# Staged rows laid out by channel group, small pieces of the experts' loads, and work moved between engines at the seams of a three-stage kernel

## The reference

```
h = concat(patches @ W + b, table[x_txt])
h = h + causal_attention(layernorm(h))
h = h + ternary_ffn(layernorm(h))                  # gelu, width 1024
x = layernorm(h); xi, z = split(x @ Win.T)         # 512 channels each
lam = exp(-8 softplus(omega) sigmoid(xi @ Wl.T + bl));  v = xi @ Wv.T + bv
h_t = lam_t (h_{t-1} - 2 v_t (v_t . h_{t-1}) / |v_t|^2) + (1 - lam_t) xi_t    # 192 steps
h = h + (silu(z) * h_t) @ Wout.T
h = h + moe(layernorm(h))     # 8 experts, 2 per token
```

## Time and profile before

| | us |
|---|---|
| median of 3 runs | 997.94 (995.04 to 998.17) |
| the profiled execution | 999.17 |
| its span, first to last instruction | 997.4 |
| TensorE busy | 942.3 (94%) |
| VectorE busy | 785.9 (79%) |
| ScalarE busy | 594.5 (60%) |
| GpSimd busy | 542.2 (54%) |
| transfers | 96.34 MB in 135878 packets, 130166 of them under 2 KB |

### The profile page before, as it was taken

How to read it: one execution, slowest core, us unless ns; L and a number is a source line. 1 busy time by engine, 2 the same in 40 slices (tenths; PEclk the granted TensorE clock), 3 DMA queues, 4 the chain that set the end, 5 groups by cost and what they waited for, 6 DMA issues and landing times. The chain is left out here.

```text
span 997.4 us, 19802 instructions
## 1 busy us (share of the span) xinstructions
PE 942.3 (94%) x6006; PEld 844.9 (85%) x6006; DVE 785.9 (79%) x2396; ACT 594.5 (60%) x1181; POOL 542.2 (54%) x662
## 2 busy tenths in 40 slices
PE   6889999999999999988799999999998999997998
PEld 6789999999999999875588888888887888876887
DVE  4877777777777777664499999999997889995776
ACT  1366666666666666563567676777664666752541
POOL 4256666666666666344355455555543446542663
PEclk9999999999999999899899999999999899999999
DMA  6001111111111141003799999999999999993210
GB/s 221 17 27 43 44 43 43 42 42 42 42 42 42 42 149 32 17 17 111 89 149 156 156 156 154 156 154 155 155 154 173 145 153 145 150 143 76 98 64 22
DMA packets 135878, 96.34 MB, mean 97 GB/s; under 512 B 12270, under 2 KB 130166, under 8 KB 135158
## 3 DMA queue, kind: packets, MB, share of 16 engines
q1 hardware_dynamic: 134262, 91.20, 53.4%
q0 software_dynamic: 1536, 4.20, 1.4%
HBM read 31.91 MB, written 13.11 MB: 45 GB/s over the span
## 5 line engine op out<-in xcount | busy, mean ns | idle before, releaser
L334 POOL TENSOR_TENSOR gelu_lo<-gelu_out,gelu_hi 128x384 fp32r<-128x384 f32 x124 | 145.6, 1200 | 34.0 <-DVE gelu_hi L549 32.1
L1036 POOL TENSOR_TENSOR B_y<-B_scan_in,B_states 128x512 f32<-128x512 f32 x48 | 61.8, 1288 | 97.8 <-ACT B_states L1110 97.8
L752 PE MATMUL psAB<-ternary_down,gelu_hi 128*128 128x256 f32 x384 | 96.7, 290 | 4.9 <-POOL gelu_lo L334 4.0
L688 PE MATMUL psAB<-x2T_hi,ternary_up 128*128 128x384 f32 x256 | 94.9, 371 | 2.5 <-DVE residual L678 2.3
L752 PE MATMUL psAB<-ternary_down,gelu_lo 128*128 128x256 f32 x384 | 93.3, 282 | 0.0
L688 PE MATMUL psAB<-x2T_lo,ternary_up 128*128 128x384 f32 x256 | 87.9, 343 | 0.0
L1284 PE MATMUL psAB<-Win_hi,B_x_hi 128*128 128x512 f32 x192 | 83.5, 435 | 0.0
L1296 PEld LDWEIGHTS psAB<-B_partial_dots,B_minus_same_batch 128*128 128x128 f32 x384 | 65.3, 191 | 18.2 <-DVE B_partial_dots L1187 9.2
L752 PEld LDWEIGHTS psAB<-ternary_down,gelu_hi 128*128 128x128 f32 x384 | 72.2, 188 | 8.9 <-POOL gelu_lo L334 7.5
L1203 DVE SCALAR_TENSOR_TENSOR psAB<-B_decayed_u,psAB 128x128 f32<-128x128 f32 x192 | 68.0, 354 | 12.7 <-PE psAB L1296 11.5
L1284 PE MATMUL psAB<-Win_hi,B_x_lo 128*128 128x512 f32 x192 | 75.7, 394 | 0.0
(11 more groups left out here) (267 smaller groups left out, 3330.4 us busy)
## 6 DMA issues: line engine op xcount, KB each, us to landing
B_scan_in<-B_stage SPq DMA_DIRECT2D x192, 256.0 KB, 6.6
patches<-in_patches SPq DMA_DIRECT2D x16, 384.0 KB, 3.1
B_residual<-layer_out SPq DMA_DIRECT2D x48, 128.0 KB, 3.5
out_dram<-B_residual SPq DMA_DIRECT2D x48, 128.0 KB, 2.8
layer_out<-residual SPq DMA_DIRECT2D x32, 128.0 KB, 1.8
raw_Win<-in_experts SPq DMA_DIRECT2D x4, 768.0 KB, 4.4
raw_Wl<-in_experts SPq DMA_DIRECT2D x4, 768.0 KB, 4.1
layer_out<-residual SPq DMA_DIRECT2D x32, 64.0 KB, 2.0
```

The source lines that it names most:

```text
L334: nc.gpsimd.tensor_tensor(act_l[:, k, :], act[:, k % DEEP, :], act_h[:, k, :].bitcast(F32), ALU.subtract).then_inc(s["ffn_lo"], 1)
L688: last = nc.tensor.matmul(out, a, b, start=(n == 0), stop=(n == len(terms) - 1))
L752: last = nc.tensor.matmul(ps[:, 6 + k // 2, (k % 2) * D:(k % 2 + 1) * D], x[:, c, k * P:(k + 1) * P], dn_w[:, c, :], start=(c == 0 and x i ...
L1036: nc.gpsimd.tensor_tensor(y[:, j % 2], ring[:, j % R_RING, :, GATE, :], hs[:, j % 2], ALU.mult).then_inc(s["y"], 1)
```

## The change

It writes `stage` as slot, channel group, quantity, channel, so that each copy into the ring reads one run of 2 KB per partition; spreads the loads for stage C over iterations 22 to 36, the two experts in four pieces each, behind the ring's copies; moves the folds (one straight behind `turn_win`, one behind up 4, six behind down 2); builds `minus` first thing in B and splits the out-projection two iterations later; warms the exponential's table at B's start and silu's in iteration 48; writes out the merged v weight earlier; computes the routing weights on GpSimd in iterations 34 and 35; sends half of the last rows through ScalarE's queue and the last store in stage C; adds ten transposes on TensorE behind B's last product; puts the routing transposes first and the bias product ahead of the last rows in C, these in bank 7; and gives half of the last expert's low part to VectorE. The diff, cut where context or waits on counts repeat:

```
@@ -174,7 +174,7 @@
-for m, behind in enumerate((("up", 2), ("up", 4), ("up", 6), ("down", 2), ("down", 2), ("down", 2), ("down", 2), ("down", 2))):
+for m, behind in enumerate((("turn_win", 0), ("up", 4), ("down", 2), ("down", 2), ("down", 2), ("down", 2), ("down", 2), ("down", 2))):
@@ -780,6 +780,7 @@
+            pe.wait_ge(s["x2_lo"], G)
@@ -973,19 +977,6 @@
     for i in range(FIRST, LAST):
-        if i == TT - 18:
-            for a, b in ((E.b_up, io["up_bias"]), (E.b_dn, io["down_bias"])):
-                sp.dma_start(a[:], b).then_inc(E.s["const_in"], 16)
-            for a, b in ((E.picked, io["picked"]), (E.weights, io["routing"])):
-                for q, lo, hi, q_in, lo_in in ((0, 0, P, 0, 0), (2, 0, P, 3, 0), (1, 0, 64, 1, 64), (1, 64, P, 2, 0),
-                                               (3, 0, 64, 1, 0), (3, 64, P, 2, 64)):
-                    sp.dma_start(a[lo:hi, q, :], b[lo_in:lo_in + hi - lo, q_in, :]).then_inc(E.s["const_in"], 16)
-            sp.wait_ge(s["w_lo"], 3)
-            sp.wait_ge(s["m_ps"], 2)
-            for e in range(2):
-                sp.dma_start(E.raw[e], io["experts"][e]).then_inc(E.s["raw_in%d" % e], 16)
@@ -1004,10 +995,10 @@
             if j == TT - 1:
-                for b in range(2):
-                    sp.dma_start(E.acc[b * (P // 2) + 60:(b + 1) * (P // 2), 3, :],
-                                 res[4 * b:4 * b + 4, j % R_RES, :]).then_inc(E.s["h_in"], 16)
-            sp.dma_start(io["out"][:, 4 * j:4 * j + 4, :], res[:, j % R_RES, :]).then_inc(stored[j % 4], 16)
+                sp.dma_start(E.acc[60:P // 2, 3, :], res[0:4, j % R_RES, :]).then_inc(E.s["h_in"], 16)
+            else:
+                sp.dma_start(io["out"][:, 4 * j:4 * j + 4, :], res[:, j % R_RES, :]).then_inc(stored[j % 4], 16)
@@ -1018,10 +1009,33 @@
-                             stage[:, j % 2, :, g * P:(g + 1) * P]).then_inc(arrived[j % 4], 16)
+                             stage[:, j % 2, g, :, :].rearrange("p w c -> p (w c)")).then_inc(arrived[j % 4], 16)
+        if i == TT - 26:
+            sp.dma_start(E.b_up[:], io["up_bias"]).then_inc(E.s["const_in"], 16)
+            sp.dma_start(E.b_dn[:], io["down_bias"]).then_inc(E.s["const_in"], 16)
+        if i in range(TT - 25, TT - 19):
+            q, lo, hi, q_in, lo_in = ((0, 0, P, 0, 0), (2, 0, P, 3, 0), (1, 0, 64, 1, 64), (1, 64, P, 2, 0),
+                                      (3, 0, 64, 1, 0), (3, 64, P, 2, 64))[i - (TT - 25)]
+            for a, b in ((E.picked, io["picked"]), (E.weights, io["routing"])):
+                sp.dma_start(a[lo:hi, q, :], b[lo_in:lo_in + hi - lo, q_in, :]).then_inc(E.s["const_in"], 16)
+        if i in range(TT - 19, TT - 11):
+            if i == TT - 19:
+                sp.wait_ge(s["w_lo"], 3)
+                sp.wait_ge(s["m_ps"], 2)
+            e, n = divmod(i - (TT - 19), 4)
+            cols = slice(n * 6 * D // 4, (n + 1) * 6 * D // 4)
+            sp.dma_start(E.raw[e][:, cols], io["experts"][e][:, cols]).then_inc(E.s["raw_in%d" % e], 16)
...
 def _(pool):
+    nc.gpsimd.memset(minus[:], 0.0).then_inc(s["minus_zero"], 1)
+    for n, apart in enumerate(range(-96, 97, 32)):
+        pool.wait_ge(s["minus_zero"], n + 1)
+        nc.gpsimd.affine_select(out=minus[:], in_=minus[:], compare_op=ALU.not_equal, fill=-1.0, base=apart,
+                                pattern=[[-1, P]], channel_multiplier=1).then_inc(s["minus_zero"], 1)
@@ -1059,23 +1073,37 @@
+        if i == TT - 14:
+            pool.wait_ge(E.s["const_in"], 224)
+            nc.gpsimd.tensor_copy(E.picked_f[:], E.picked[:]).then_inc(E.s["cast"], 1)
+            nc.gpsimd.tensor_scalar(E.b_up_one[:], E.b_up[:, :, 2:4], 1.0, None, ALU.add).then_inc(E.s["b_up_one"], 1)
+            pool.wait_ge(E.s["cast"], 1)
+            for e in range(E_N // 2):
+                nc.gpsimd.tensor_scalar(E.eq[:, :, :, e], E.picked_f[:].rearrange("p q k -> p k q"), float(e), None,
+                                        ALU.is_equal)
+        if i == TT - 13:
+            for e in range(E_N // 2, E_N):
+                last = nc.gpsimd.tensor_scalar(E.eq[:, :, :, e], E.picked_f[:].rearrange("p q k -> p k q"), float(e),
+                                               None, ALU.is_equal)
+            last.then_inc(E.s["eq"], 1)
+            pool.wait_ge(E.s["eq"], 1)
+            nc.gpsimd.tensor_tensor(E.wc[:], E.eq[:, 0], E.eq[:, 1], ALU.add).then_inc(E.s["eq_sum"], 1)
+            pool.wait_ge(E.s["eq_sum"], 1)
+            nc.gpsimd.tensor_tensor(E.wc[:], E.wc[:], E.weights[:], ALU.mult).then_inc(E.s["wc"], 1)
+            pool.wait_ge(E.s["wc"], 1)
+            nc.gpsimd.tensor_scalar(E.wc_scaled[:], E.wc[:], 1.0 / ALPHA, None, ALU.mult).then_inc(E.s["wc_scaled"], 1)
...
-        if i == -4:
+        if i == -2:
...
-            nc.gpsimd.memset(minus[:], 0.0).then_inc(s["minus_zero"], 1)
-            for n, apart in enumerate(range(-96, 97, 32)):
-                pool.wait_ge(s["minus_zero"], n + 1)
-                nc.gpsimd.affine_select(out=minus[:], in_=minus[:], compare_op=ALU.not_equal, fill=-1.0, base=apart,
-                                        pattern=[[-1, P]], channel_multiplier=1).then_inc(s["minus_zero"], 1)
...
 def _(sc):
-    nc.scalar.activation(warm[:], ones[:, 0:1], ACT.Tanh)
+    nc.scalar.activation(warm[:], ones[:, 0:1], ACT.Exp)
@@ -1086,6 +1114,7 @@
+    merged(2)
@@ -1144,21 +1173,24 @@
+            merged(3)
...
-            merged(2)
-            merged(3)
...
-            nc.scalar.activation(stage[:, j % 2, U, :], ps[:, bank("v", j), :], ACT.Copy,
+            nc.scalar.activation(stage[:, j % 2, :, U, :], by_group(ps[:, bank("v", j), :]), ACT.Copy,
...
-            nc.scalar.activation(stage[:, j % 2, LAM, :], u2[:], ACT.Exp).then_inc(s["lam"], 1)
+            nc.scalar.activation(stage[:, j % 2, :, LAM, :], by_group(u2[:]), ACT.Exp).then_inc(s["lam"], 1)
...
+        if i == TT:
+            nc.scalar.activation(warm[:], ones[:, 0:1], ACT.Silu)
+    sc.wait_ge(s["res"], TT)
+    sc.dma_start(E.acc[P - 4:P, 3, :], res[4:8, (TT - 1) % R_RES, :]).then_inc(E.s["h_in"], 16)
@@ -1218,8 +1250,8 @@
-            nc.vector.scalar_tensor_tensor(out=stage[:, j % 2, GATE, :], in0=th_z[:], scalar=1.0,
-                                           in1=ps[:, bank("z", j), :], op0=ALU.add,
+            nc.vector.scalar_tensor_tensor(out=stage[:, j % 2, :, GATE, :], in0=by_group(th_z[:]), scalar=1.0,
+                                           in1=by_group(ps[:, bank("z", j), :]), op0=ALU.add,
@@ -1238,6 +1270,8 @@
+        if i == -5:
+            merged(2)
@@ -1251,19 +1285,18 @@
         if i == -4:
-            for n in range(2, 4):
-                merged(n)
+            merged(3)
...
             if j == 0:
-                nc.vector.tensor_scalar(stage[:, 0, LAM, :], stage[:, 0, LAM, :], first[:], None,
+                nc.vector.tensor_scalar(stage[:, 0, :, LAM, :], stage[:, 0, :, LAM, :], first[:], None,
...
-            nc.vector.scalar_tensor_tensor(out=stage[:, j % 2, DRIVE, :], in0=stage[:, j % 2, LAM, :], scalar=1.0,
-                                           in1=ps[:, bank("xi", j), :], op0=ALU.subtract,
+            nc.vector.scalar_tensor_tensor(out=stage[:, j % 2, :, DRIVE, :], in0=stage[:, j % 2, :, LAM, :], scalar=1.0,
+                                           in1=by_group(ps[:, bank("xi", j), :]), op0=ALU.subtract,
@@ -1366,6 +1399,8 @@
+    for _ in range(10):
+        nc.tensor.transpose(ps[:, bank("v", TT - 1), 0:P], ident[:], ident[:])
@@ -1401,6 +1433,8 @@
 def _(sp):
+    last_tile = T // 4 - 1
+    sp.dma_start(io["out"][:, T - 4:T, :], E.res[:, last_tile % 12, :]).then_inc(E.stored[last_tile % 4], 16)
@@ -1433,7 +1467,8 @@
-        nc.gpsimd.tensor_tensor(a_l[:, e % 2, :, :], glu[:], a_h[:, e % 2, :, :].bitcast(F32),
+        part = slice(0, 1) if e == E_N - 1 else slice(0, 2)
+        nc.gpsimd.tensor_tensor(a_l[:, e % 2, part, :], glu[:, part, :], a_h[:, e % 2, part, :].bitcast(F32),
@@ -1459,38 +1494,30 @@
-        sc.wait_ge(s["act"], 2 * e + 2)
...
-        nc.scalar.activation(a_h[:, e % 2, :, :], glu[:], ACT.Copy).then_inc(s["a_hi"], 1)
+        if e == E_N - 1:
+            sc.wait_ge(s["act"], 2 * e + 1)
+            nc.scalar.activation(a_h[:, e % 2, 0, :], glu[:, 0, :], ACT.Copy).then_inc(s["a_hi"], 1)
+            sc.wait_ge(s["act"], 2 * e + 2)
+            nc.scalar.activation(a_h[:, e % 2, 1, :], glu[:, 1, :], ACT.Copy).then_inc(s["a_hi_last"], 1)
+        else:
+            sc.wait_ge(s["act"], 2 * e + 2)
+            nc.scalar.activation(a_h[:, e % 2, :, :], glu[:], ACT.Copy).then_inc(s["a_hi"], 1)
...
 def _(v):
-    v.wait_ge(s["const_in"], 224)
-    nc.vector.tensor_copy(picked_f[:], picked[:]).then_inc(s["cast"], 1)
-    v.wait_ge(s["cast"], 1)
-    for k in range(2):
-        for e in range(E_N):
-            last = nc.vector.tensor_scalar(eq[:, k, :, e], picked_f[:, :, k], float(e), None, ALU.is_equal)
-    last.then_inc(s["eq"], 1)
-    v.wait_ge(s["eq"], 1)
```

(36 more changed lines are left out.)

20 lines of the change are left out of this document (11 added, 9 removed).

## The result

The kernel after takes 979.83 us, the median of four runs (979.02 to 981.79), against 997.85 (995.04 to 998.17) before in the same session; the ratio is 0.9828, 95% interval 0.9806 to 0.9851. The forecast was 978.0, in a range of 973.5 to 985. The profiled execution took 979.70 us with a span of 977.8; that of before had 999.17 and 997.4.

What follows compares the result with a forecast made beforehand. No single limit overall: VectorE's 8.55 us per tile sets the steady scan, leaving the load burst and seams. Terms 1.8 + 6.8 + 8.3 - 0.2 + 2.9 + 0.7 = 20.3 us gave 978 us, range 973.5 to 985.

Steps and rivals of the forecast that it cites:

- End of A: Last group of stage A: moved folds and a kept-up TensorE clock start stage B 1.8 us earlier, ends 0.3 and 3.
- Prologue: Start of stage B: earlier value norm, no TensorE idle and clock at 2.4 GHz gain 6.8 us, ends 4 and 8.
- Staged rows: Ring copies in the scan: 2 KB runs land in about 3 us instead of 6.6, gaining no time by themselves.
- the first rival: Ring copies land no sooner in 2 KB runs; 0.6 us late in each of eight iterations, 983 us; chance 0.10.
- Burst: Loads for stage C during the scan: spreading them removes VectorE's 6.15 us idle and its ripple, 8.3 us gained.
- Routing on GpSimd: Thirteen small operations in two scan iterations make the product with the states and write-back late, costing 0.2 us.
- B to C: Seam into stage C: C starts 1.35 us earlier, and expert 1 starts 2.9 us earlier in all, ends 1.4 and 3.5.
- The clock's 1.4: Start of C: ten transposes shorten TensorE's idle to about 0.7 us, winning 1.4 us of clock.
- Last expert: End of stage C: splitting the low parts over two engines ends TensorE's 0.79 us wait, 0.7 us gained.
- The third rival: VectorE's stage writes slow down in four runs; 1042 us if they take twice their time; chance 0.03.
- the fourth: Merged exponential and tanh table isn't one set, or the warmed silu is displaced; 979 us at a seam; chance 0.02.

Runs made afterwards that it cites:

- e4: Kernel after with the weight folds in stage A's last group back at their old places; 979.75 us in one execution.
- e3: Kernel after with the prologue's old order restored (mask, warming activation, output-projection merge); 984.51 us, ratio 0.9874 to the kernel before.
- e7: Kernel before with only the staged rows laid out by channel group (2 KB runs); 995.85 us, ratio 1.0002 to the kernel before.
- e6: Separate kernel without the computation: sets of four 256 KB on-chip copies, and VectorE operations; 10.1 us a set into 32 partitions, 4.4 into 128, in 2 KB runs.
- e1: Kernel after with the old layout of the staged rows (512 B runs); 1001.38 us, ratio 1.0066 to the kernel before.
- e11: e1 with an unused tile of 416 B a partition put in front of stage B's tiles; 981.37 us, ratio 0.9845 to the kernel before.
- e2: Kernel after with biases, routing arrays and first two experts' inputs again loaded in one lump; 991.07 us, ratio 0.9937 to the kernel before.
- e12: e10 without the ten transposes on TensorE ahead of stage C; 982.04 us, ratio 0.9869 to the kernel before.
- e10: Kernel after with an unused tile of 416 B a partition in front of stage B's tiles; 979.97 us, ratio 0.983 to the kernel before.

## Why the prediction held, and where it didn't

**End of A, 1.8.** The pair of profiles shows 1.7, but for another reason than the folds: 0.2 is theirs (e4), the rest is one execution's fall of the clock. The step took one profiled clock for a property of the code. That the number came out is luck.

**Prologue, 6.8.** Right in its mechanism, 6.0 in size: mask, value norm, no idle, no clock at 0.51. What failed is "where a stall goes": I named nothing that would be late next. The ring copies were, and with them the third and fourth tile: 3.0 of the 6.0 are lost again in the first five tiles. e3 puts the worth of the part at 3.2 by its stages and 4.7 by the medians.

**Staged rows.** "No time in the scan comes of that itself" was right for the part alone (e7). "Landing in about 3 us" was wrong: 6.9. The comparison with the patches' 3.1 us was between copies into 32 and into 128 partitions, and e6 shows that this alone makes a factor of 2.3 within on-chip memory; that the patches come from HBM is not told apart by any run. So the first rival's first sentence, that the copies land no sooner, was true, and its price was wrong: 0.6 us late for each of eight pieces, of which none came, as the marks 8.53 us apart show. What the part did bring I had not seen: it covers nearly all of the cost of the new places, which is 20 us with short runs (e1 against e11).

**Burst, 8.3.** Right in place and size: 8.5 (e2).

**Routing on GpSimd, -0.2.** No wait at its iterations. But its five tiles are what moved stage B's: the step counted instructions and not the memory that they take.

**B to C, 2.9.** 1.0 and 1.6 in place of 1.35 and 1.55. ScalarE's issue took 1.19 us where I had taken 0.62 to 0.7, and lies on the path. The clock's 1.4 is confirmed by e12 at 1.5.

**Last expert, 0.7.** 0.1. The wait of the earlier trace rows, 0.79 us, went, but TensorE has two others, 0.45 and 0.25 us. GpSimd's split of weights and VectorE's product of two on-chip inputs meet:

```profile
917.53 4.37 DVE L1550 SCALAR_TENSOR_TENSOR C_glu<-C_up,C_silu 128x512 f32<-128x512 f32 x2
...
925.62 1.29 DVE L1550 SCALAR_TENSOR_TENSOR C_glu<-C_up,C_silu 128x512 f32<-128x512 f32 x2 [1.07 <-POOL C_act_lo L1471]
```

```profile
934.07 0.50 PE L1573 MATMUL psC<-Wl_Win_hi,C_w_hi 128*128 128x512 f32 x1 [0.45 <-POOL C_w_lo L1456]
```

The same two operations take 4.37 us beside GpSimd's 3.5 us split and 1.29 alone, and TensorE waits 0.45 us. The two halves of the last low parts are on these two engines as well.

**The third rival** (writes in four runs) did not come, nor the fourth: one table load at the start of B and silu's at 896.68, none between.

**The sum.** 20.3 was forecast, 19.6 is the difference of the two spans. Of that 4.4 is chance in stage A and some 1.4 the clock at its end, so the parts of the change explain 13.8. The medians differ by 18.0 in the first session and by 15.6 between before and e10 in the session of e10. Between 2 and 4 us are left that the stages of these two executions don't place. So the time came out within 2 us of the forecast partly by luck: the burst was right, prologue, last expert and A brought less, and the base had been a long execution: 999.17 us, where the medians of before on the other chips are 994.14 to 996.82.

## What to carry to other kernels

Ask of a change not only what its instructions cost but which tiles its buffers move: print the places before and after, and try an unused tile in front if a transfer gets longer for no reason. Judge a part by taking it away from the whole as well as by adding it alone: the layout was worth 0 alone, 21 here, and with the tiles at other places 1.4 here, which may be nothing. When a stall at the head of a pipeline goes, the next thing late is the buffer with the fewest slots; and what one profiled clock shows at a short idle stretch is not yet the code's: look for the same stretch in several executions.

## What had not been expected of the hardware

- Packets of ring copies took some 10% (512 B) and up to 5% (2 KB) longer in the mean when the tiles stood 96 B past a multiple of 256 B; with short runs the kernel lost 20 us by it.
- Four copies of 256 KB took 10.1 us into 32 partitions each and 4.4 into 128, each with 2 KB runs.
- VectorE with two on-chip inputs went from 692 to 1466 ns beside GpSimd.
- A DMA issue on ScalarE took 1.19 us, two 1.50; on SyncE four took 2.5 to 3.4.
- An idle stretch of 1.64 us of TensorE had a fall of the clock behind it in one execution of three.
- With the same code and no change near it, the clock fell between 410 and 413 us in six of thirteen executions, and these came to the last transposes of stage A at 429.5 to 431.7 us, the others at 427.1 to 428.6.
